# Routing the tokens of an expert layer in two parts, and one program instead of two

## What is computed

```python
x = x + cross_attention_0(layernorm(x), ctx, ...)
x = x + ternary_ffn_0(layernorm(x), ...)
x = x + block_1(layernorm(x), ctx, ...)   # self-attention "a1", cross-attention "a2",
                                          # each with a feed-forward of 256 -> 1024 -> 256
# the last step, on xf = layernorm(x) as 2048 rows of 256:
logits  = xf @ Wg + bg                                   # Wg: 256 x 8
one_hot = jax.nn.one_hot(jnp.argmax(logits, axis=-1), e)
h   = gelu(einsum('td,edh->eth', xf, W1))                # W1: 8 x 256 x 1024
y   = einsum('eth,ehd->etd', h, W2)                      # W2: 8 x 1024 x 256
out = x + einsum('etd,te->td', y, one_hot)
```

## Time and profile before

| | us |
|---|---|
| median of 3 runs | 1157.76 |
| lowest and highest of them | 1154.86, 1159.51 |
| the profiled execution | 1160.95 |
| its span from the first to the last instruction | 1159.2 |

### The profile page before, as it was taken

How to read it: one execution, slowest core, us unless ns; L and a number is a source line. 1 busy time by engine, 2 the same in 40 slices (tenths; PEclk the granted TensorE clock), 3 DMA queues, 4 the chain that set the end, 5 groups by cost and what they waited for, 6 DMA issues and landing times. The chain is left out here.

```text
span 1159.2 us, 20650 instructions
## 1 busy us (share of the span) xinstructions
PE 1056.4 (91%) x8642; PEld 727.7 (63%) x8642; DVE 527.4 (45%) x1201; ACT 459.0 (40%) x659; POOL 272.2 (23%) x408
## 2 busy tenths in 40 slices
PE   5999974998999998999999999999999994999997
PEld 3555642554456555565766575666667663999996
DVE  5566678886347777752422333665233113000000
ACT  3757543666344444444123225554221222222221
POOL 3022301000013333323022001555311103222211
PEclk9999997999999999999999999999999995999999
DMA  8500000000051000000000020000612104856510
GB/s 248 79 2 2 2 1 0 1 1 1 1 129 18 2 2 2 2 2 1 1 1 0 1 91 1 3 2 22 197 36 81 47 19 147 327 190 196 178 55 1
DMA packets 55342, 60.55 MB, mean 52 GB/s; under 512 B 23587, under 2 KB 47055, under 8 KB 55250
## 3 DMA queue, kind: packets, MB, share of 16 engines
q1 hardware_dynamic: 52306, 52.93, 14.9%
q0 software_dynamic: 2944, 6.30, 1.8%
HBM read 54.76 MB, written 7.21 MB: 53 GB/s over the span
## 5 line engine op out<-in xcount | busy, mean ns | idle before, releaser
L648 DVE TENSOR_REDUCE small<-ps 128x16 f32<-128x1920 f32 (+1 forms) x64 | 142.2, 2221 | 62.4 <-PE ps L1271 41.0
L988 ACT ACTIVATE r_a<-ps 120x1024 f32<-120x1024 f32 (+1 forms) x128 | 124.1, 1021 | 23.8 <-PE ps L1306 23.5
L1373 PE MATMUL ps<-r_w,r_k 128*128 128x256 f32 x512 | 113.3, 381 | 1.6 <-ACT r_k L1145 1.6
L1588 PE MATMUL ps<-r_a,r_w 128*128 128x512 f32 x256 | 111.5, 593 | 3.1 <-ACT r_a L1063 3.1
L1373 PEld LDWEIGHTS ps<-r_w,r_k 128*128 128x128 f32 x512 | 96.3, 190 | 17.1 <-issue 2.9
L1324 PE MATMUL ps<-r_a,onesf 128*32 128x256 f32 (+1 forms) x768 | 90.5, 385 | 8.2 <-ACT r_a L988 8.2
L1819 PEld LDWEIGHTS ps<-feat_block,w_block 128*128 128x128 f32 x736 | 87.9, 196 | 1.5 <-ACT feat_block L1913 0.4
L1819 PE MATMUL ps<-feat_block,w_block 128*128 128x128 f32 x736 | 88.2, 280 | 0.0
L1588 PEld LDWEIGHTS ps<-r_a,r_w 128*128 128x128 f32 x256 | 48.4, 190 | 61.6 <-issue 57.4
L1905 DVE TENSOR_TENSOR rows_block<-ps,rows_block 128x256 f32<-128x256 f32 x23 | 9.8, 424 | 166.1 <-PE ps L1831 166.1
L1831 PE MATMUL ps<-w_all,hidden_block 128*128 x368 | 83.1, 379 | 0.0
(11 more groups left out here) (232 smaller groups left out, 1762.9 us busy)
## 6 DMA issues: line engine op xcount, KB each, us to landing
w_block<-in_L_ffn_W SPq DMA_DIRECT2D x23, 1024.0 KB, 6.0
w_all<-in_L_ffn_W SPq DMA_DIRECT2D x8, 1024.0 KB, 9.5
r_w<-in_L_xattn_a_li_w SPq DMA_DIRECT2D x4, 1024.0 KB, 7.3
x_all<-in_x SPq DMA_DIRECT2D x4, 512.0 KB, 7.2
x_rows<-x_all SPq DMA_DIRECT2D x4, 512.0 KB, 3.0
x_rows<-r_a SPq DMA_DIRECT2D x4, 512.0 KB, 3.0
y_all<-in_L_ffn_w_gate SPq DMA_DIRECT2D x1, 1024.0 KB, 11.1
y_all<-in_L_ffn_w_up SPq DMA_DIRECT2D x1, 1024.0 KB, 13.3
```

The source lines that it names most:

```text
L648: step(dve.tensor_reduce(nm.rearrange("p (j s) -> p j s", j=4), src, AX.X, ALU.max, negate=True))
L988: act.activation(PT[0:nk, 2 * x:2 * x + 2, :], bank(n % 2, 2 * x, 2)[0:nk], ACT.Exp, scale=scale).then_inc(sem["exp_done"], 1)
L1373: ins_ = pe.matmul(o[:, t // 2, (t % 2) * D:(t % 2 + 1) * D], src[:, c, t * P:(t + 1) * P], w[:, c, :], start=(c == 0), stop=(c == chunks ...
L1588: ins_ = pe.matmul(o, LI[a]["li2"][:, c, m * P:(m + 1) * P], FT3[:, c, :], start=(c == 0), stop=(c == KC - 1))
```

## The change

1. **Two routes.** After the third pair's experts are chosen, twelve tiles are known. At least five blocks can be filled with them alone: 1536 tokens, of which at most 127 in each of eight experts are left over, is 5 full blocks or more (`EARLY` = 5). `counts(0)`, `places(0)`, `slot_tokens(0)` and `slots(0)` route these; `counts(1)` and so on route all that is left once the fourth pair is chosen, into the other 18 blocks (`LATER`). The number of blocks stays 23.
2. **PE's order.** The last pair's `up` is cut into 3, 2, 2 and 1 pieces. Between them stand the transposes and the gate of the third pair and `counts(0)`; `slot_tokens(0)` stands between the halves of `ff_down`. After `ff_down` come block 0's transposes, then the last pair's transposes, gate and `counts(1)`, mixed with `block_up(0)` and `block_up(1)`. `slot_tokens(1)` stands after `block_down(1)`.
3. **The last gate** is one piece of four tiles again, not two halves.
4. **POOL** issues gathers 0 and 1 ahead of the last pair's first `rstd(2)`, gathers 2 to 4 ahead of the second, and gathers 5 to 7 after scatters 0 and 1. The five tables of constants (iota) are made during pair 1.
5. **SP** loads W1 of blocks 0 to 3 as soon as `block_ei` has the early experts, ahead of the last pair's stores; blocks 4 and later wait for the end of `ff_down`, since their buffers lie on memory in use, and block 5 also for the second route.
6. **ACT** loads the table of the experts' gelu right after the last `hidden`. The eight passes that fill the row buffers with zeros are gone, and the `own_ids` table is made on DVE.
7. **One program.** The barrier and the second block are gone; the routing's and blocks' tiles are views of memory that the layers no longer use (`r_a`, `r_w`, `bvec`, `max_rows`), so names in the order below differ: before `rows_block`, after `bvec` and `r_a`.
8. The block transposes write one PSUM bank (6) for all blocks, not two in turn.

The core of the diff:

```diff
+EARLY_TILES = TILES - TILES // (B // 2)
+EARLY = -(-(EARLY_TILES * P - E * (P - 1)) // P)
+LATER = BLOCKS - EARLY
...
+                for p in range(NP - 1):
                     sp.wait_ge(sem["x5_ready"], p + 1)
+                    rows_store(p, "x5_stored", 0)
...
+                sp.wait_ge(es["experts_known"], 1)
+                sp.wait_ge(sem["li1_done"], 2 * NP)
+                for b in range(4):
+                    expert_weights(b)
+                sp.wait_ge(sem["x5_ready"], NP)
+                rows_store(NP - 1, "x5_last_stored", 0)
+                sp.wait_ge(sem["xh_half"], 2)
+                rows_store(NP - 1, "x5h_last_stored", 1)
+                sp.wait_ge(sem["dn_done"], 2 * NP)
+                for b in range(4, BLOCKS):
+                    if b == EARLY:
+                        sp.wait_ge(es["experts_known"], 2)
+                    expert_weights(b)
...
+                pool.wait_ge(sem["x5_stored"], 16 * (NP - 1))
+                pool.wait_ge(sem["x5h_stored"], 16 * (NP - 1))
+                pool.wait_ge(es["slots_ready"], 1)
+                gather(0)
+                gather(1)
+                rstd(2)
+                for b in range(2, EARLY):
+                    gather(b)
+                rstd(2)
+                for b in range(BLOCKS):
+                    scatter(b)
+                    if b == 1:
+                        pool.wait_ge(es["slots_ready"], 2)
+                        pool.wait_ge(sem["x5_last_stored"], 16)
+                        pool.wait_ge(sem["x5h_last_stored"], 16)
+                        for k in range(EARLY, ROWS):
+                            gather(k)
...
+                def places(k):
+                    r, later = ROUTES[k], k == 1
+                    v, n, nb = r.eight, r.tiles, r.blocks
+                    dve.wait_ge(es["counts_done"], k + 1)
+                    total, ahead = r.counts[:, n * E:(n + 1) * E], r.counts[:, 0:n * E].rearrange("p (t e) -> p t e", e=E)
...
+                    route_step(dve.tensor_scalar(r.first_of, r.first_of, -MAGIC, float(P), ALU.add, ALU.mult))
+                    route_step(dve.scalar_tensor_tensor(r.lane_of, r.pos, half, r.first_of, ALU.add, ALU.subtract))
+                    route_step(dve.tensor_tensor(r.hit, block_row[:, 0:nb].rearrange("p (o n) -> p o n", o=1).to_broadcast([P, n, nb]),
+                                                 r.first_of.rearrange("p (t o) -> p t o", o=1).to_broadcast([P, n, nb]), ALU.is_equal))
+                    dve.tensor_tensor(r.tile_ids, r.hit, tile_row[:, 0:n, 0:nb], ALU.mult)
+                    dve.tensor_scalar(r.own_ids, r.hit, own_no, None, ALU.mult)
+                    for t in range(n):
+                        ins_ = dve.tensor_scalar(r.lanes[:, t, :], lane_no, r.lane_of[:, t:t + 1], None, ALU.is_equal)
+                    ins_.then_inc(es["lanes_ready"], 1)
...
                 choose(NP - 2)
+                places(0)
+                slots(0)
...
                 choose(NP - 1)
+                places(1)
+                expert_rows(0)
+                expert_rows(1)
+                slots(1)
+                for b in range(2, BLOCKS):
+                    expert_rows(b)
...
+                features(0)
+                last_copy(0)
+                gelu(0, range(1))
+                last_copy(1)
+                features(1)
+                gelu(0, range(1, 2))
+                for b in range(1, BLOCKS):
+                    gelu(b)
+                    if b + 1 < BLOCKS:
+                        features(b + 1)
...
+                def counts(k):
+                    o, n = ROUTES[k].counts, ROUTES[k].tiles
+                    pe.wait_ge(sem["chosen"], NP - 1 + k)
+                    pe.matmul(o, strict[:], onehot[:, 0:n + 1, :].rearrange("p t e -> p (t e)"), start=True, stop=False)
+                    for t in range(n):
+                        ins_ = pe.matmul(o[:, (t + 1) * E:(n + 1) * E], onesb[:], onehot[:, t:t + 1, :].to_broadcast([P, n - t, E]),
+                                         start=False, stop=(t == n - 1))
+                    ins_.then_inc(es["counts_done"], 1)
+                def slot_tokens(k):
+                    r = ROUTES[k]
+                    pe.wait_ge(es["lanes_ready"], k + 1)
+                    for t in range(r.tiles):
+                        for j, ids in enumerate((r.own_ids, r.tile_ids)):
+                            ins_ = pe.matmul(r.ids, r.lanes[:, t, :], ids[:, t, :], start=(t == 0 and j == 0),
+                                             stop=(t == r.tiles - 1 and j == 1))
+                    ins_.then_inc(es["ids_done"], 1)
...
+                pe.wait_ge(sem["lg_ready"], NP - 2)
+                ff_transposes(NP - 1, "a2")
+                up(NP - 1, "a2", range(0, 3))
+                pe.wait_ge(sem["xhq_ready"], 2 * NP - 1)
+                pe.wait_ge(sem["ft3_ready"], 2 * NP)
+                transpose_rows(ps[:, 2:4, :], XHQ).then_inc(sem["xqT_done"], 1)
+                up(NP - 1, "a2", range(3, 5))
+                pe.wait_ge(sem["ftq_ready"], 2 * NP - 1)
+                gate(ps[:, 2, :], range(PT_TILES)).then_inc(sem["logits_done"], 1)
+                up(NP - 1, "a2", range(5, 7))
+                pe.wait_ge(sem["xb_ready"], 2 * NP)
+                counts(0)
+                up(NP - 1, "a2", range(7, 8))
+                hidden_at["a2", NP - 1] = pieces
+                ff_down(NP - 1, "a2", range(0, 2)).then_inc(sem["dn_half"], 1)
+                slot_tokens(0)
+                ff_down(NP - 1, "a2", range(2, 4))
+                pe.wait_ge(sem["x5_half"], 1)
+                block_transposes(0)
+                last_transposes(0)
+                pe.wait_ge(es["slots_ready"], 1)
+                pe.wait_ge(sem["lg_ready"], NP - 1)
+                block_up(0)
+                last_transposes(1)
+                block_transposes(1)
+                block_up(1, range(1))
+                pe.wait_ge(sem["fq_half"], 2)
+                pe.wait_ge(sem["x5_ready"], NP)
+                gate(bank(1, 3), range(PT_TILES)).then_inc(sem["logits_done"], 1)
+                block_up(1, range(1, 2))
+                block_transposes(2)
+                counts(1)
+                pe.wait_ge(w2_loaded, 16 * E)
                 pe.wait_ge(es["experts_known"], 1)
-                pe.wait_ge(es["slots_ready"], 1)
-                pe.wait_ge(w2_loaded, 16 * E)
-                transposes(0)
-                transposes(1)
-                up(0)
                 for b in range(BLOCKS):
-                    if b + 1 < BLOCKS:
-                        up(b + 1)
-                    if b + 2 < BLOCKS:
-                        transposes(b + 2)
-                    down(b)
...
+                    if b >= 1:
+                        if b + 1 < BLOCKS:
+                            block_up(b + 1)
+                        if b + 2 < BLOCKS:
+                            block_transposes(b + 2)
+                    if b == EARLY:
+                        pe.wait_ge(es["experts_known"], 2)
+                    block_down(b)
+                    if b == 1:
+                        slot_tokens(1)
...
-        nc.all_engine_barrier(sem_only=True)
```

424 lines of the change are left out of this document (187 added, 237 removed).

## The result

The changed kernel takes 1138.42 us (median of four runs, 1135.74 to 1140.59) where the kernel before takes 1156.42 beside it (1154.86 to 1159.51). The ratio is 0.983, with a 95% interval of 0.982 to 0.985: 17.0 to 21.3 us less. A second set of runs gave 1139.52 and 0.984 (0.982 to 0.986). The forecast was 1137.5.

The account below looks back on a forecast made before the run. PE, busy 91% of the span, was taken as the bound, losing time in tail waits and low clock. First `down` 22.0 us sooner, less 1.8 for `slot_tokens(1)`, leaves 20.2: 1157.76 becomes 1137.5 us; range 1133 to 1145.

Parts of the forecast that it names:

- The stretch: PE from the start of the last pair's `up` to the first `down`: 46.2 us at the upper clock.
- `slot_tokens`: PE's slot matmuls: `slot_tokens(0)` 1.3 us within `ff_down`, `slot_tokens(1)` 1.8 us between blocks.
- Gather 0: POOL's gather for block 0: starts near 952.1, lands after 4.34 us at 956.4, wanted at 957.8.
- rival 1: Tail before the first `down`: gather 0 or a half 1 to 3 us late, clock falls; 1141 to 1146, chance 0.14.
- First route: DVE's routing chain for the third pair's choice: ends near 947.5, PE asks at 949.6; two us to spare.
- The second half: Last half's layer norm after `ff_down`: rows normed at 962.1, PE there near 962.2; called even.
- Second route: Routing after `counts(1)`: gathers 5 to 7 landed near 989, wanted near 994; five us to spare.
- Behind the first `down`: PE streams 23 blocks, 159.03 us as before, plus `slot_tokens(1)` at 1.8.
- the largest gain: Low end of the range: all new waits at nothing and both slot groups at their lower bound, 22.5 us.
- Rival 3: Block 0 starts only after the last pair's routing: some 4 us won, 1154; chance 0.04 together with others within half a percent.
- Rival 2: POOL's in-order queue: block 5's rows come after 994 and PE stands amid the blocks; 1142 to 1150, chance 0.05.
- Rival 4: Clock falls in the new tail and stays down; with 60 us low the time is 1167, chance 0.03.

Follow-up runs that it names:

- w1_behind_rows: Changed kernel, with SP loading W1 of blocks 2 and 3 only after the rows of blocks 0 and 1 have landed; 1136.5 us, ratio 0.981.
- before_warm_fit: Kernel before, with unread matmuls added in PE's waits in groups of 5, 1, 2, 13 and 11 `warm`; 1157.39 us, ratio 0.999.
- before_warm: Kernel before, with 56 unread matmuls of 256 columns meant for PE's waits between the last gate and block 0; 1160.18 us, ratio 1.003.
- route_late: Changed kernel, with `slot_tokens(1)` behind the `down` of block 2, not block 1, and `slots(1)` on DVE behind it; 1142.25 us, ratio 0.987.
- blocks_late: Changed kernel, with transposes and `up` of blocks 0 and 1 behind the last pair's transposes and gate on PE and ACT; 1143.23 us, ratio 0.989.
- before_warm_six: Kernel before, with unread matmuls added in PE's waits in groups of 5, 1, 2, 13 and 6 `warm`; 1154.71 us, ratio 0.998.

## Why the prediction was right, step by step

It forecast 1137.5 us and the runs gave 1138.4 and 1139.5. By S, free of the head, it forecast a gain of 20.2 and there were 20.56. The medians alone show less, 18.0 and 17.6 (the kernel before had 1157.08 beside the second set), in intervals that hold 20.2. That the time came so near to 1137.5 has some luck in it: the forecast took off from a median of 1157.76, and with the fourth run the kernel before stood at 1156.42, from which 20.2 less is 1136.2.

- **The stretch: 46.2 forecast, 46.58 measured.** Two errors of nearly one size and opposite sign are in it, which is luck. The gather's wait was not in the sum: 0.85, and some 0.15 more by the starts, since `ff_down` takes 13.97 up to the transposes where nothing waits (`w1_behind_rows`) and 15.0 here. `slot_tokens(0)` took 0.60 and not 1.3. From the first block's transposes to the first `down` it is 12.96 us, where the terms for it (0.66, 1.26, 7.14, 1.85, 0.6, 1.05 and 0.3) give 12.86. ACT's copy was 0.87, as in the earlier trace rows.
- **`slot_tokens` was the mis-sized term.** 0.60 and 0.81 us (from its start to that of the next group) against 1.3 and 1.8. The step took half of the 2.58 us in the earlier trace rows for the clock's, and kept the other half as PE's own. The runs show that neither the clock nor PE set the 2.58: at the upper clock, with DVE's steps beside it, the group takes 2.57 (`before_warm_fit`), and with nearly all steps done 0.96 (`before_warm`). DVE's 16 steps of 2.69 us set the pace. The lower bounds, 1.0 and 1.3, were no bounds.
- **Gather 0 was the step that failed.** That the 4.34 us of before had the loads of W1 in full flow beside them, as now, was wrong: the old order had a wait in SP's code that held the third load back until the rows were there, and the change dropped it. The same wait is in the 22.38 us of the earlier trace rows, which the prediction divided by eight; four loads without it were out in 3.85 us and not in 11. PE got the rows 6.66 us after the gather's start, where 4.34 were forecast. The forecast named this margin the least of all, though its own numbers give 1.4 us here and 0.1 for the second half; a part of rival 1 came true, with 0.85 us, at which the clock did not fall.
- **The other margins.** First route: DVE's steps ended at 942.53, PE asked at 944.88: 2.35 to spare, 2 forecast. The second half was called even; its rows were normed at 956.28 and asked for at 958.22, 1.9 to spare. Counted from the last pair's `up`, the rows were ready 1.2 us sooner than I had it (36.4 and not 37.6, since POOL's gathers began 0.6 to 0.9 sooner), and PE asked 0.7 later, mostly by the gather's wait. The rows of DVE's `apply`:

```profile
950.58 0.73 DVE L711 TENSOR_SCALAR r_a<-x_all,small 128x256 f32<-128x256 f32 x2 [3.08 <-POOL small L495]
...
955.55 0.73 DVE L711 TENSOR_SCALAR r_a<-x_all,small 128x256 f32<-128x256 f32 x2 [1.11 <-POOL small L495]
```

  Second route: 5 us forecast, 6.5 by `route_late`.
- **The clock** stayed at 1.00 between the two, as forecast, and `blocks_late` shows that this was no matter of course: within a wait of 3.27 us it fell, to 0.56 in the two us from 954 on and 0.50 in the next.
- **Behind the first `down`**: 160.8 forecast, 160.03 measured, because `slot_tokens(1)` takes 0.81 and not 1.8; the order of the blocks cost nothing.
- **The range's low end.** The 22.5 us of "the largest gain" do not come out of the terms: with all new waits at nothing (0.87, 1.05 and 0.3) and both slot groups at their lower bounds it is 23.2. It changes nothing in the argument.
- **"Nothing ahead of 924 differs"** is right of PE's work and wrong of the times. The head alone moves by over 5 us between executions. The span of the two profiles would have given the change 25 us.
- **Rival 3** (early blocks not early) is refuted by the first profile. Rival 2 did not occur in the changed kernel, where PE has no wait for rows behind the first `down`; `route_late` shows how far off it was. Rival 4 did not occur either.

## What to carry to other kernels

Where an engine waits at a point that depends on the last part of the data, split the decision: what is sure from the earlier parts can be worked on in just those waits, and it pays twice where the stall also pulled the clock down, as in `blocks_late`. When code is moved, look also for the waits that it leaves behind; one that seemed to guard a buffer had kept a latency-critical gather clear of bulk loads. And measure a change of 1 or 2% between two marks in the trace that enclose it, not by the span.

## What was not expected of the hardware

- The head of the program, with the same work for PE each time, took 919.0 to 924.7 us over twelve profiles. The difference is in the granted clock between 100 and 300 us (0.91 and 0.94 in one, 0.94 and 0.98 in another), where PE is busy about 75% and 94% of the time. From 300 to 900 us the clock is 1.00 and PE's busy time 573.40 to 573.51 us in all twelve.
- The clock fell within a single wait of 3.27 us (`blocks_late`). Around the end of 2.57 us in which PE was recorded as busy with 32 small matmuls that DVE paced it fell in `before_warm_fit` (0.61 in the window 972 to 974, then 0.50), and it stayed at 1.00 behind the same instructions in `before_warm_six`. It held through waits of 0.85, 1.10 and 0.77.
- A gather of 128 rows released PE 4.47 and 3.60 us after its start behind two loads of 1 MB (`before`, `before_warm_six`), and 6.66 and 6.92 us behind four (the changed kernel, twice).
- Small bf16 matmuls follow each other in 0.025 us: 24 of 128x5 in 0.60, 32 of 128x18 in 0.81.
